# A two-layer graph kernel on one core: count moved into the second aggregation, column mean from weighted degrees, attention table inside the attention's block, gates handed out between tiles

## The reference

```
x += segment_sum(w * LN(x)[src], dst) @ W0.T + b0                  # L0 graph layer
x += scale * expert[argmax(LN(x) @ gate)](LN(x)), 8 experts        # L0 expert layer, 256-1024-256, relu
agg = segment_sum(w * (LN(x) @ W1)[col], row) + bias               # L1 graph layer: edges turned round
x += relu((agg - mean) * rsqrt(var + eps) * gamma + beta)          #   mean, var over the nodes, by column
h = LN(x) @ W_gat                                                  # L1: attention gives the gates of 4 experts
e = leaky_relu(a_src[src] + a_dst[dst]); alpha = softmax of e over each dst (with self loops)
scores = mean over heads of LN(segment_sum(alpha * h[src], dst) + b_gat)
x += sum over top 2 experts of softmax(score) * expert(LN(x))      # 256-512-256, gelu
```

## Time and profile before

| | us |
|---|---|
| median of 3 runs | 8170.69 (8167.85 to 8171.03) |
| the profiled execution's own time | 8178.54 |
| its span | 8176.8 |
| PE busy | 5609.0 (69%) |
| DVE busy | 4610.6 (56%) |
| POOL busy | 4954.2 (61%) |
| ACT busy | 3659.7 (45%) |

### The profile page before, as it was taken

The page is one execution under the profiler, slowest core; times in us unless marked ns, Lnnn a source line. Parts: engine busy times, 40 slices in busy tenths (PEclk is TensorE's granted clock), DMA queues, the critical chain, the costliest instruction groups (busy, mean ns, idle before and its releaser), DMA issues. The chain is left out here.

```text
span 8176.8 us, 89733 instructions
## 1 busy us (share of the span) xinstructions
PE 5609.0 (69%) x20059; PEld 4148.2 (51%) x20059; DVE 4610.6 (56%) x9158; ACT 3659.7 (45%) x9403; POOL 4954.2 (61%) x4772
## 2 busy tenths in 40 slices
PE   6555555555557999954455555555565899999967
PEld 4344444444455666633344444444455566666646
DVE  6455555555577999937544444444558344443334
ACT  3566666666632222213366666666632222222224
POOL 4777777777732222223377777777744777777741
PEclk9777777777757999977677777777785999999978
DMA  5333344333331111135333333333324322222246
GB/s 151 107 113 113 113 115 114 111 103 101 102 112 61 52 42 57 42 76 161 109 103 103 103 103 104 103 103 103 101 69 142 78 62 59 63 65 59 64 131 236
DMA packets 500791, 798.74 MB, mean 98 GB/s; under 512 B 123215, under 2 KB 365500, under 8 KB 500188
## 3 DMA queue, kind: packets, MB, share of 16 engines
q0 software_dynamic: 200736, 454.79, 21.2%
q1 hardware_dynamic: 299552, 338.23, 12.9%
HBM read 596.91 MB, written 197.30 MB: 97 GB/s over the span
## 5 line engine op out<-in xcount | busy, mean ns | idle before, releaser
L828 PE MATMUL part<-rows,spread 128*128 x6656 | 2292.8, 519 | 1751.8 <-SPq L768 1536.0
L828 PEld LDWEIGHTS part<-rows,spread 128*128 128x128 f32 x6656 | 1760.0, 271 | 2282.1 <-issue 1914.4
L807 DVE TENSOR_TENSOR agg<-agg,part 128x256 f32 x3328 | 1403.0, 422 | 1885.0 <-PE part L828 1558.9
L790 POOL DMA_INDIRECT rows<-f,row x1568 | 1568.1, 1000 | 515.3 <-issue 477.7
L790 POOL DMA_INDIRECT rows<-h,row x1568 | 1537.7, 981 | 506.4 <-issue 477.7
L847 ACT ACTIVATE spread<-iota,place 128x128 f32<-128x128 f32 x3328 | 1017.0, 388 | 1545.9 <-PE part L828 1448.2
L1743 POOL DMA_INDIRECT rows<-gat,src x1122 | 1093.9, 975 | 369.2 <-issue 338.7
L853 ACT ACTIVATE spread<-spread,weight 128x128 f32<-128x128 f32 x3328 | 1017.2, 388 | 13.7
L1808 PE MATMUL hid_ps<-agg,w 128*128 128x512 f32 (+1 forms) x1600 | 692.3, 585 | 49.5 <-DMA b<-in_L_ffn_b 49.5
L1819 PE MATMUL y_ps<-agg,hid 128*128 128x256 f32 x3136 | 708.4, 379 | 0.0
L400 POOL COPY spare<-pay 128x1024 f32<-128x1024 f32 x105 | 222.4, 2119 | 734.0 <-DVE pay L387 505.6
(11 more groups left out here) (382 smaller groups left out, 6117.0 us busy)
## 6 DMA issues: line engine op xcount, KB each, us to landing
expert_rows<-y_all SPq DMA_DIRECT2D x196, 256.0 KB, 2.2
made<-expert_rows SPq DMA_DIRECT2D x49, 1024.0 KB, 7.2
x<-x SPq DMA_DIRECT2D x42, 896.0 KB, 7.9
rows<-f,row POOLq DMA_INDIRECT x1568, 2.8
rows<-h,row POOLq DMA_INDIRECT x1568, 2.8
rows<-gat,src POOLq DMA_INDIRECT x1122, 2.4
xbuf<-zero SPq DMA_DIRECT2D x128, 128.0 KB
x<-xbuf SPq DMA_DIRECT2D x32, 512.0 KB, 4.9
```

Of the source, the lines that this page charges most:

```text
L790: pool.indirect_dma_start(out=rows[:, u, :], out_offset=None, in_=table, in_offset=bass.IndirectOffsetOnAxis(ap=q.row[:, c:c + 1], axis=0) ...
L807: nc.vector.tensor_tensor(sum_t, sum_t, part[:, p % NB, 0:D], ALU.add).then_inc(added, 1)
L828: nc.tensor.matmul(part[:, p % NB, 0:D], spread[:, p % (2 * BANKS), :], row_p, start=True, stop=True).then_inc(multiplied, 1)
```

## The change

Nine edits are made together.

1. `FILLED`: both aggregations issue and await 1563 gathers (200,000 edges) in place of 1568.
2. The first aggregation carries a 257th column of ones, so `agg` also receives the weighted degree of every node; `route_first` copies it to `k.degree`. `update_experts` gains 98 matmuls `total(t)` (degree column times h1 tile) and one ScalarE copy: the column mean of the second aggregation, `k.mean`. The second aggregation starts its `agg` from bias - (mean + bias) in place of 0. `normalize_nodes` loses the sums, the mean and the centring; squares of 8 groups stay with ScalarE and TensorE, those of 6 groups go to VectorE. `layer_norm_in` keeps 6 buffers `f` in place of 8.
3. The count becomes a class `Tally` and moves into groups 8 to 178 of the second aggregation, one instruction of 1536 elements for each step in place of two of 768; the goals are loaded and split in two halves. One PSUM bank of eight goes to it.
4. `pack_attention` is merged into the block of `pair_arrays`; a store and a plan's store are no longer awaited at once.
5. `run_experts`: `plan_sums` stands ahead of the second-layer products of the last block.
6. `update_experts`: four `y` buffers, ScalarE scales three groups ahead, at tile 3 of a group in place of two ahead at tile 0.
7. The small loads of the attention and of the mixing are made in one `load_small` ahead of the second aggregation.
8. `attention_table` is merged into `attend`; the expert weights have a semaphore for each expert; the table's store is issued behind the weights of experts 0 and 1; GpSimd waits for it.
9. `mix_experts`: `gates` is a generator whose pieces are handed out, one behind each mixed tile from the first of a turn; ScalarE's Sqrt and Exp come at tiles 6 and 12.

The core of the diff:

```diff
+FILLED = -(-EDGES // P)
+ECH = -(-FILLED // LANES) * LANES
...
+def tally_rows(nc, dve, c, n):
+
+    if n >= 2:
+        dve.wait_ge(c.tallied, n - 1)
+    m, at = len(c.cols(n)), c.cols(n)[0]
+    nc.vector.tensor_tensor(c.hot[:, n % 2, 0:m, :, :].rearrange("p c d (i t) -> p (c d) i t", t=2),
+                            bc(c.places[:, :].rearrange("p (i t) -> p i t", t=2), 2 * m, 1),
+                            bc(c.fields[:, at:at + m, :, :].rearrange("p c d t -> p (c d) t"), P // 2, 2), ALU.is_equal).then_inc(c.hot_done, 1)
...
+def tally_counts(nc, pe, c, n):
+
+    pe.wait_ge(c.hot_done, n + 1)
+    for col in c.cols(n):
+        h = c.hot[:, n % 2, col % c.COLS, :, :]
+        ins = nc.tensor.matmul(c.count_ps, h[:, 1, :], h[:, 0, 0:TILES], start=col == 0, stop=col == GCH - 1)
+    ins.then_inc(c.tallied, 1)
...
+def aggregate_edges(nc, k, table, q, agg, begun, w, first, last, clear, words=None, bias=None, last_i=None):
...
+    WIDE = D + 1 if begun else D
...
+        NB = BANKS if last_i is None else BANKS - 1
...
+                for i in range(FILLED):
...
+                    pool.indirect_dma_start(out=rows[:, u, 0:D], out_offset=None, in_=table,
...
-                    nc.vector.memset(agg[:, :, :], 0.0).then_inc(ready, 1)
...
+                    for g in range(GROUPS):
+                        link(nc.vector.tensor_copy(agg[:, g * GROUP:(g + 1) * GROUP, :], bc(centre[:, :], GROUP, 1)))
...
                 for g in range(groups):
                     add(g)
+                    n = g - Tally.FIRST
...
+                    if c is not None and 0 <= n < c.STEPS:
+                        tally_rows(nc, dve, c, n)
...
                     sort_on_vector(nc, dve, w, share(g), share(g + 1), sort_ps)
...
+                def total(t):
+                    nc.tensor.matmul(mean_ps, k.degree[:, t:t + 1], res[t // GROUP % 2][:, t % GROUP, :], start=t == 0, stop=t == TILES - 1).then_inc(meaned, 1)
...
-                    if j == 0 and g + 2 < GROUPS:
-                        weigh(g + 2)
...
+                    if j == 3 and g + 3 < GROUPS:
+                        weigh(g + 3)
...
+                    if g == NB - 1:
+                        plan_sums(nc, pe, k, r.columns)
                     for q in range(4):
...
-                plan_sums(nc, pe, k, r.columns)
...
-                for g in range(GROUPS):
-                    nc.vector.tensor_tensor(group(g), group(g), bc(mean[:, :], GROUP, 1), ALU.add).then_inc(centred, 1)
...
+                for g in range(BY_ACT, GROUPS):
+                    link(nc.vector.tensor_tensor((partial if g == BY_ACT else own)[:, :, :], group(g), group(g), ALU.mult))
...
-                    if 1 <= m <= TALLIES:
-                        tally(m - 1)
...
+                pool.wait_ge(indexed, 1)
+                pool.wait_ge(table_in, 16)
...
-                    if t % M == GROUP and t // M + 1 < TURNS:
-                        gates(t // M + 1)
...
+                    if t % M == 0:
+                        ahead = gates(t // M + 1) if t // M + 1 < TURNS else iter(())
                     dve.wait_ge(summed, t + 1)
                     nc.vector.scalar_tensor_tensor(x[:, t, :], made[t // 2 % YB][:, t % 2, 0:D], gate[:, t, 0:1], sum_ps[t % R][:, 0:D],
...
+                    next(ahead, None)
```

More of the change, by code:

```diff
@@ new lines, in tally_runs, with tally_bases @@
+def tally_runs(nc, dve, link, c):
+    dve.wait_ge(c.tallied, c.STEPS)
+    link(nc.vector.tensor_scalar(c.counts[:, :], c.count_ps, 1.0, None, ALU.add))
+    link(nc.vector.tensor_tensor_scan(c.ends[:, :], c.counts[:, :], c.counts[:, :], 0.0, ALU.add, ALU.bypass))
+    link(nc.vector.tensor_tensor(c.ends[:, :], c.ends[:, :], c.counts[:, :], ALU.subtract))
+    dve.sem_inc(c.run, 1)
+def tally_bases(nc, pe, k, c):
+    pe.wait_ge(c.run, 1)
+    nc.tensor.matmul(c.last_ps, k.before[:, :], c.counts[:, :], start=True, stop=False)
+    nc.tensor.matmul(c.last_ps, k.ones[:, :], c.ends[:, :], start=False, stop=True).then_inc(c.based, 1)
@@ L785, in _ @@
             def _(pool):
[L786 to L791, removed]
+                for i in range(FILLED):
+                    u = i % SPAN
+                    if i >= SPAN and u % BANKS == 0:
+                        pool.wait_ge(freed, (i - SPAN) // BANKS + 1)
+                    pool.indirect_dma_start(out=rows[:, u, 0:D], out_offset=None, in_=table,
+                                            in_offset=bass.IndirectOffsetOnAxis(ap=q.row[:, i:i + 1], axis=0)).then_inc(gathered[u], 16)
             @block.vector
@@ L817, in _ @@
             def _(pe):
+                if not begun:
+                    nc.tensor.matmul(part[:, 0, 0:D], k.ones[0:1, :], k.mean[:, :], start=True, stop=True).then_inc(shown, 1)
+                pe.wait_ge(ready, 1)
                 slots = [pe.alloc_register(f"slot{n}_{nc.next_id()}") for n in range(BANKS)]
@@ L915, in route_first @@
     B = 5
+    agg = sums[:, :, 0:D]
     with Stage(nc) as s:
@@ L1218, in _ @@
                     ins.then_inc(multiplied, 1)
+                    if t >= 2:
+                        total(t - 2)
+                for t in range(TILES - 2, TILES):
+                    pe.wait_ge(made, t + 1)
+                    total(t)
             @block.scalar
@@ L1828, in _ @@
                     results(m, n, h)
-                    if 1 <= m <= TALLIES:
-                        tally(m - 1)
-                pe.wait_ge(run, 1)
-                nc.tensor.matmul(last_ps, k.before[:, :], counts[:, :], start=True, stop=False)
-                nc.tensor.matmul(last_ps, k.ones[:, :], ends[:, :], start=False, stop=True).then_inc(based, 1)
                 pe.wait_ge(tail_done, 1)
```

436 lines of the change are left out of this document (233 added, 203 removed).

## The result

The changed kernel takes 7920.15 us (median of 4 runs, 7918.03 to 7921.00) against 8170.14 us for the kernel before (4 runs). The ratio is 0.9694, 95% interval 0.9677 to 0.9711: 3.1% faster. The forecast was 7893 us in 7850 to 7970. The profiled execution took 7921.0 us, its span is 7919.3, 257.5 less than the span before. The median stands 27 us above the forecast: 20 of them are the sum's, 7 come from the step from the profiled execution to the median (7.8 us taken off; it is 0.9 here). Four of the later kernels ran on a chip where the kernel before takes 9707 us, 19% more; nothing of those four is compared with the rest.

A forecast was written before the change was run, and what follows sets the result against it. GpSimd's gather issue bounds the second aggregation, TensorE the attention with GpSimd close behind, gate stalls slow the mixing, VectorE the update stage. Terms sum to -277.5 us from 8178.5: 7901, less 7.8 to the median, 7893 (7850 to 7970).

The forecast's parts named there:

- TensorE under 97%: Attention: sign that GpSimd has taken over, TensorE busy under 97% with waits that end in gathers.
- The count in the second aggregation: Second aggregation: 171 compares on VectorE slow GpSimd's gathers, +21 us; with fewer gathers and a wait, the stage gets +16.
- 0.12 us for each microsecond: Second aggregation: gather delay per microsecond of two-input SBUF compares, from 50 us excess over some 408 us of compares.
- The update stage and what follows: Update stage up to the second aggregation: earlier scaling -47 us, small loads +2.3, merged key block -10.8.
- The attention: Attention: without the count's 165 us on TensorE, GpSimd takes over with 1406 us of gathers; -108 us.
- Rival C: Attention: gathers stay at 1.303 us each, gain only 51 us; kernel time 7950 us, chance 0.08.
- The normalisation: Normalisation: squares start at once, so var comes some 30 us after the start; -46 us.
- The mixing: Mixing: turns no longer stall for new gates, 11.3 us saved a turn; -68 us.
- Rival D: Mixing: DMA holds at 311 GB/s or below, gain 20 to 30 us; kernel time 7935 us, chance 0.10.
- B: Second aggregation: gathers lose the full 1.0 us to each of 171 compares; kernel time 8042 us, chance 0.07.
- E: Second aggregation: compare is VectorE's wall; from 3.8 us each the change loses, at 4.0 kernel time 8201 us; chance 0.03.
- F: Any stage: an edit does nothing, for example late gates pieces still stall turns; +68 us, kernel time 7961 us, chance 0.06.

The follow-up runs named there:

- 8: Changed kernel plus idle matmuls in the attention that feed nothing: 7937.5 us with 1026 of them, 7966.6 us with 14 for each of 171 halves.

## Why the prediction was right, and where its size was off

**What bounds the kernel.** Right at each place where a run looked: the aggregation by GpSimd's issue (no wait for a buffer in any of these runs), the attention by TensorE before and GpSimd after, the stalls of the mixing by the gates alone. One sign was a poor one: "TensorE under 97%" came true on the mean only (1345.5 of 1404 us busy from 6266 to 7670, 96%), and in single windows TensorE stayed at 100%. The busy share does not tell the two limits apart; the added work of 8 does.

**The count in the second aggregation** is the term that was mis-sized: +21 us for the compares, 41.3 measured. The mechanism, VectorE's two-input SBUF instructions delaying GpSimd's gathers, was right. The failed step is "0.12 us for each microsecond", in two ways. Its divisor was wrong: the sort's compares take 255 us in that stage of the kernel before (L381 and L382, 153 pairs of 0.69 us each and 18 pairs of 1.22 us each), not "some 408 us"; the 50 us of excess then make 0.20 for each microsecond, and the term +35. And such a rate is no constant: the same work cost 0.25 for each microsecond at the group's end, 0.15 behind the third add and 0.03 in halves, by how much of an instruction is left when a gather begins. Of the 20 us, 6 came back, for without the compares the stretch is 12.1 us shorter than before, where 6.4 were forecast.

The Trainium skill (GPSIMD Engine Reference, Specifications) states that VectorE instructions with two SBUF inputs contend with GpSimd; the traces here agree. The 176 us that the prediction gave for complete contention took every compare to hold a gather for its whole length; in fact 138 gathers began inside the 171 compares and were held for 0.44 us on the mean, and the sort's compares behind them held 17 us less than without the count.

**The update stage and what follows:** -45.3 for -55.5. The wait went as forecast (48.5 us from first to last L1288, forecast 51). What failed is to take TensorE's "98 small matmuls, 2.8 us a group" as hidden work: it is hidden in the steady state, but not behind VectorE's last operation, where 14 tiles at 1.75 us in place of 1.09 make 9.3 us. Deferring the last 14 of them gave back 4.2. The small loads and the merged key block gave -6.0 in place of -8.5: VectorE waited 10.69 us for the iota behind the gathers, and the last key operations stood ahead of the first turn.

**The attention:** the stretch from the first gather to the store of the last block became 104.5 us shorter, forecast 103; 1122 gathers took 1404.7 us, forecast 1406. The start gained 0.2 in place of 5, as the table's landing grew from 13.4 to 16.8 us behind the weights. Rival C (gathers stay at 1.303) is out, and its premise, that their mean was "no compare's doing", does not hold: of the 34.2 us that the gathers of this stage took above 0.945 us each before, 19.6 fell on those that began inside the count's compares, and 5.4 are left in all.

**The normalisation:** -44.3 for -46, squares at 3.02 us a group as before.

**The mixing:** -75.5 for -68. Rival D is out: the 311 GB/s between stalls were the demand, not the limit; 397 to 412 were moved. That bound should have been read from what waits (nothing waited for `made`), not from the share.

**Rivals B, E and F.** The whole price of B was 171 us, a quarter of it came. E's compare takes 0.95 us, by its own terms far from 3.8; this agrees with what the Trainium skill states of 16-bit operands (Vector Engine (DVE) Microarchitecture Reference, 5.1), that in inner runs of more than one element they go two a cycle; here the runs are of two elements. F is out for the three edits taken back, 14, 60 and 76 us; the others were not taken back one by one.

The sum was 20 us too low: 13.6 of the aggregation, 10.2 of the update stage and 5 of the attention's start, against 7.5 of the mixing and 1 of the rest.

## What to carry to other kernels

When GpSimd's gathers set the pace, cut VectorE's two-input SBUF instructions into short pieces and look in the timeline at which of them a gather begins inside: the same 162 us of compares cost 41, 25 or 5 us by their place and length alone. Place and length were changed together for the 5, so what each gives is not told apart. A small job put into the steady state of a pipeline is hidden there but not in its last groups; count the tail apart. And a stage's saving ends at the second limit: 165 us of TensorE work left the attention, and 105 came out, because GpSimd's gathers stood at 1431 of 1462 us.

## What the runs showed of the hardware that I had not expected

A gather that begins while VectorE runs an instruction with two SBUF inputs takes longer by what is left of that instruction, less 0.13 us (1483 of 1484 gathers, within 0.02 us); a gather that has begun is not lengthened by an instruction that starts behind it. It is held for one instruction and not for the row: in the earlier trace rows L381 ends at 6006.21 and the held gather at 6007.03, while L382 runs beside it (6006.25 to 6007.48). This is also why the doubled compare added only 9.4 us: 171 gathers began inside one, but some 50 of them within 0.05 us of its start, and these were not held.

The count's bfloat16 matmul took 0.161 us in the kernel before (84 in 13.5) and takes 0.07 in the changed one (six in 0.42), like those with contiguous operands in the idle work. The one-hot matrices lay with a stride of six elements before and lie contiguous now; that the stride is the cause was not tried apart.
